# Token products as single float32 products in column strips, coefficients in three bfloat16 parts, with a new table of steps

## The reference, cut to what matters

```python
x = x + 0.5 * ffn(layernorm(x))
x = x + attn(layernorm(x))
x = x + 0.5 * ffn(layernorm(x))

def ffn(x):                                  # x: 4096 tokens x 128
    scores = sigmoid(x @ gate.T)             # 8 experts
    # best of two groups, best two experts in it, coefficients made to sum to 1
    lat = x @ fc1_w.T
    routed = sum over the two experts e of coefficient * (relu2(lat @ w1[e].T) @ w2[e].T) @ fc2_w.T
    return routed + relu2(x @ up_w.T) @ down_w.T      # shared part, 512 wide

def attn(x):                                 # 16 heads of 8
    q, k, v = x @ qkv_w.T                    # q and k turned by position (rotary)
    w = softmax(q @ k.T * SCALE + alibi)
    return (w @ v) @ proj_w.T + proj_b
```

## Time and profile before

| | |
|---|---|
| time, median of 3 runs | 744.61 us (744.25 to 746.72) |
| the profiled execution: its own time | 749.13 us |
| the profiled execution: span of the core | 747.3 us |
| PE busy | 678.4 us (91%) |
| ACT busy | 534.5 us (72%) |
| DVE busy | 436.0 us (58%) |
| POOL busy | 200.2 us (27%) |
| granted TensorE clock, mean | 0.971 |

### The profile page before, as it was taken

The page is one execution under the profiler, slowest core; times in us unless marked ns, Lnnn a source line. Parts: engine busy times, 40 slices in busy tenths (PEclk is TensorE's granted clock), DMA queues, the critical chain, the costliest instruction groups (busy, mean ns, idle before and its releaser), DMA issues.

```text
span 747.3 us, 18920 instructions
## 1 busy us (share of the span) xinstructions
PE 678.4 (91%) x7798; PEld 365.2 (49%) x7798; DVE 436.0 (58%) x1167; ACT 534.5 (72%) x461; POOL 200.2 (27%) x174
## 2 busy tenths in 40 slices
PE   5996999999999989899999999998989899878977
PEld 3884634454454545355535545454445344423556
DVE  4679354667667567648478663673565353424544
ACT  3686487878679677687786695867877787767614
POOL 1116223232432512322425243131132211201130
PEclk9999599999999999999999999999999999988979
DMA  8013512132046140305112301324222000020100
GB/s 263 1 29 112 150 33 68 49 90 61 28 124 155 50 118 6 95 27 142 35 32 51 92 19 44 104 54 108 49 49 62 5 20 6 11 63 6 38 16 19
DMA packets 41024, 46.38 MB, mean 62 GB/s; under 512 B 9186, under 2 KB 27210, under 8 KB 40802
## 3 DMA queue, kind: packets, MB, share of 16 engines
q1 hardware_dynamic: 39122, 43.70, 21.3%
q10 hardware_dynamic: 1808, 1.39, 0.6%
HBM read 25.48 MB, written 19.32 MB: 60 GB/s over the span
## 4 chain that ended last, share of the span: by engine, by line
PE 46%; ACT 15%; DVE 3%; issue 2%; POOL 0%; POOLq 0%; DVEq 0%; ACTq 0%
ACT weights L1415 15%; PE f_acc L1054 13%; PE f_scores L1032 10%; PE f_bank_h L1004 9%; PE f_bank_o L1181 7%; PE f_bank_c L1158 1%; PE f_bank_h L1082 1%; PE f_bank_h L1217 1%; DVE weights L1810 1%; PE f_bank_c L1123 1%; PE f_bank_c L1125 1%; PE f_acc L1181 0%; PE f_bank_c L1134 0%; PE f_bank_h L1113 0%; PE f_scores L1004 0%
## 5 line engine op out<-in xcount | busy, mean ns | idle before, releaser
L1415 ACT ACTIVATE weights<-f_scores 128x2048 f32<-128x2048 f32 (+3 forms) x213 | 394.2, 1851 | 95.8 <-PE f_scores L1032 92.5
L1054 PE MATMUL f_acc<-weights,v_res 128*9 128x512 f32 (+7 forms) x1888 | 230.5, 567 | 2.9 <-DVE f_o_out L1796 2.0
L1032 PE MATMUL f_scores<-q_op,k_full 25*128 25x512 f32 (+8 forms) x1328 | 115.9, 395 | 32.9 <-ACT weights L1415 27.7
L1181 PEld LDWEIGHTS f_bank_o<-w_out,f_hid 128*32 128x32 f32 (+1 forms) x3424 | 109.5, 114 | 73.6 <-issue 70.2
L1810 DVE TENSOR_TENSOR weights<-weights,ediag 128x512 f32<-128x512 f32 x128 | 93.4, 735 | 72.3 <-ACT weights L1415 67.2
L1181 PE MATMUL f_bank_o<-w_out,f_hid 128*32 128x128 f32 (+1 forms) x3424 | 129.0, 276 | 0.0
L1453 POOL TENSOR_TENSOR f_hid<-f_hid,f_relu 128x512 f32<-128x512 f32 x52 | 73.9, 1423 | 161.2 <-DVE f_hid L1669 161.1
L1032 PEld LDWEIGHTS f_scores<-q_op,k_full 25*128 25x128 f32 (+1 forms) x1328 | 56.0, 186 | 108.9 <-ACT weights L1415 74.2
L1453 POOL TENSOR_TENSOR f_hid<-f_relu 128x512 f32<-128x512 f32 x52 | 57.1, 1099 | 166.0 <-ACT f_relu L1328 163.8
L1328 ACT ACTIVATE f_relu<-f_bank_h 128x512 f32<-128x512 f32 x106 | 63.3, 597 | 42.8 <-PE f_bank_h L1004 42.7
L1004 PE MATMUL f_bank_h<-xn_t,w_hi 128*128 128x512 f32 x224 | 85.5, 464 | 3.0 <-DVE xn_t L1569 1.4
(11 more groups left out here) (243 smaller groups left out, 729.0 us busy)
## 6 DMA issues: line engine op xcount, KB each, us to landing
q_parts<-f_parts SPq DMA_DIRECT2D x24, 256.0 KB, 3.0
k_parts<-f_parts SPq DMA_DIRECT2D x24, 256.0 KB, 3.5
q_op<-q_parts SPq DMA_DIRECT2D x48, 96.0 KB
k_full<-k_parts SPq DMA_DIRECT2D x48, 96.0 KB
o_scratch<-f_o_out SPq DMA_DIRECT2D x124, 18.0 KB
x_ln<-in_L_attn_x_dram SPq DMA_DIRECT2D x8, 256.0 KB, 3.9
rope<-const_rope SPq DMA_DIRECT2D x1, 2048.0 KB, 9.2
x_scratch<-f_res SPq DMA_DIRECT2D x8, 256.0 KB, 2.4
```

Source lines behind the costliest of these rows:

```text
L1032: last = nc.tensor.matmul(scores[:, j, at + lo:at + hi], k_full[rows, g, kt * P:(kt + 1) * P], q_op[rows, g, CHUNK * half + lo:CHUNK * hal ...
L1054: last = nc.tensor.matmul(acc[BLOCK * j:BLOCK * j + VW, 0:piece.width], v_res[:, c // HALVES, piece.kt, col:col + VW], weights[:, n % WEIG ...
L1181: last = nc.tensor.matmul(made[strip, t * P:(t + 1) * P], hid[:, m, t * P + strip.start:t * P + strip.stop], w_out[:, m, :], start=(m == 0 ...
L1415: nc.scalar.activation(weights[:, n % WEIGHTS, :, 0:width], scores[:, :, 0:width], ACT.Exp).then_inc(exps_done, 1)
```

## The change

1. A token product is one float32 product, with one copy of the weights (`w_in`) and one of the tokens, in four column strips. The helper `product` makes it. The hidden products, those of queries, keys and values, the gate, the output projection, the spread and all output products (also those of the first two jobs and the last one, which were not cut into strips before) go through it.
2. The low part of the tokens falls away: `take_low` and `take_low2` on DVE, the low copies of the weights in the preparation, and the product of two exponentials (L1575), since the gate's logits come in one piece.
3. The coefficients are spread from three bfloat16 parts (24 rows) in place of two rounded 32-bit parts (16 rows). DVE has two more operations for them, and PE turns them by a bfloat16 product with an identity in place of a transpose.
4. The table of steps is new in all rows.

```diff
-            def times_weights(out, col, x_t):
-
-                for i, (w, part) in enumerate(((w_hi, 0), (w_hi, 1), (w_lo, 0))):
-                    last = nc.tensor.matmul(out, w[:, col:col + P], x_t[:, part, :], start=(i == 0), stop=(i == 2))
+            def product(out, still, moving, start=True, stop=True):
+
+                for strip in STRIPS:
+                    last = nc.tensor.matmul(out[strip, :], still[:, strip], moving, start=start, stop=stop,
+                                            skip_group_check=True)
                 return last
...
                 for t in range(TILES):
-                    at, cols = 2 * EXPERTS * t, slice(t * P, (t + 1) * P)
-                    nc.tensor.matmul(logits[:, at:at + 2 * EXPERTS], x_t[:, 0, cols], w_gate[:, :],
-                                     start=True, stop=False, skip_group_check=True)
-                    last = nc.tensor.matmul(logits[:, at:at + EXPERTS], x_t[:, 1, cols], w_gate[:, 0:EXPERTS],
-                                            start=False, stop=True, skip_group_check=True)
+                    last = product(logits[:, EXPERTS * t:EXPERTS * (t + 1)], x_t[:, t * P:(t + 1) * P], w_gate[:, :])
...
                 for t in range(TILES):
-                    last = nc.tensor.transpose(bank_c[0:2 * EXPERTS, t * P:(t + 1) * P],
-                                               coef_parts[:, t, :].bitcast(F32), ident[:, :])
+                    last = nc.tensor.matmul(bank_c[0:COEF_ROWS, t * P:(t + 1) * P], coef_parts[:, t, :], ident_rows[:, :],
+                                            start=True, stop=True)
...
-                times_weights(hidden_bank(job, m), IN_COL + m * P, normed_t(job)).then_inc(hid_made, 1)
+                at = IN_COL + m * P
+                product(hidden_bank(job, m), w_in[:, at:at + P], normed_t(job)).then_inc(hid_made, 1)
...
-                nc.tensor.matmul(spread_bank(job, m), spread_rows[:, m * P:(m + 1) * P], coef_t[:, :],
-                                 start=True, stop=True).then_inc(spread, 1)
+                product(spread_bank(job, m), spread_rows[:, m * P:(m + 1) * P], coef_t[:, :]).then_inc(spread, 1)
...
-                copy(normed_t(job)[:, 0, :], turn_bank(job)).then_inc(xt_high, 1)
+                copy(normed_t(job), turn_bank(job)).then_inc(xt_ready, 1)
...
-            def take_low(job):
-                dve.wait_ge(xt_high, job.index + 1)
-                v.tensor_tensor(normed_t(job)[:, 1, :], turn_bank(job), normed_t(job)[:, 0, :],
-                                ALU.subtract).then_inc(xt_ready, 1)
...
+                v.tensor_tensor(coef_rest[:, :, :], coef[:, :, :], coef_parts[:, :, 0:EXPERTS], ALU.subtract)
                 v.tensor_tensor(coef_parts[:, :, EXPERTS:2 * EXPERTS], coef[:, :, :], coef_parts[:, :, 0:EXPERTS],
-                                ALU.subtract).then_inc(coef_ready, 1)
+                                ALU.subtract).then_inc(coef_split, 1)
+                dve.wait_ge(coef_split, job.index + 1)
+                v.tensor_tensor(coef_parts[:, :, 2 * EXPERTS:COEF_ROWS], coef_rest[:, :, :],
+                                coef_parts[:, :, EXPERTS:2 * EXPERTS], ALU.subtract).then_inc(coef_ready, 1)
...
-    ("C", 3, dict(front=(355, 359, 360), norm=(361, 365, 366, 368), route=(369, 371, 371, 372, 373), coef=374,
+    ("C", 3, dict(front=(356, 359, 360), norm=(363, 366, 366, 367), route=(368, 368, 368, 368, 368), coef=374,
```

More of the change, by code:

```diff
@@ L810, in normed_t @@
         def normed_t(job):
-            return twin_xn_t if job.twin else xn_t[:, :, :]
+            return twin_xn_t[:, :] if job.twin else xn_t[:, :]
         def relu_tile(job, m):
@@ L1081, in project @@
                 for t in range(TILES):
-                    last = nc.tensor.matmul(bank_h[:, t * P:(t + 1) * P], o_in[rows, t * P:(t + 1) * P], proj_t[rows, :],
-                                            start=True, stop=True)
+                    last = product(bank_h[:, t * P:(t + 1) * P], o_in[rows, t * P:(t + 1) * P], proj_t[rows, :])
                 last.then_inc(proj_made, 1)
@@ L1179, in outputs @@
                 for t in (2 * side, 2 * side + 1):
-                    for strip in ([slice(0, P)] if job.head or job.ends else STRIPS):
-                        last = nc.tensor.matmul(made[strip, t * P:(t + 1) * P],
-                                                hid[:, m, t * P + strip.start:t * P + strip.stop], w_out[:, m, :],
-                                                start=(m == 0 and t == (2 * side if job.ends else 0)), stop=(m == HT - 1),
-                                                skip_group_check=True)
+                    last = product(made[:, t * P:(t + 1) * P], hid[:, m, t * P:(t + 1) * P], w_out[:, m, :],
+                                   start=(m == 0 and t == (2 * side if job.ends else 0)), stop=(m == HT - 1))
                 if side == 1:
@@ L1215, in value @@
                 for t in (2 * side, 2 * side + 1):
-                    for i, (part, w) in enumerate(((0, w_hi), (1, w_hi), (0, w_lo))):
-                        last = nc.tensor.matmul(v_bank(job)[:, t * P:(t + 1) * P], xn2_t[:, part, t * P:(t + 1) * P],
-                                                w[:, col:col + DIM], start=(i == 0), stop=(i == 2))
+                    last = product(v_bank(job)[:, t * P:(t + 1) * P], xn2_t[:, t * P:(t + 1) * P], w_in[:, col:col + DIM])
                 if side == 1:
@@ L1700, in norm2_centre @@
                 last.then_inc(norm2_ready, 1)
-            def take_low2(job):
-                dve.wait_ge(xt2_high, job.chunk + 1)
-                v.tensor_tensor(xn2_t[:, 1, :], out_bank(job), xn2_t[:, 0, :], ALU.subtract).then_inc(xt2_ready, 1)
             def rotary_product(job, i):
@@ L1849, in token @@
                     (last_residual if job.ends else residual)(job)
-                if step == job.at["take_low"]:
-                    take_low(job)
                 if not job.head and step == job.at["take_coef"]:
                     take_coef(job)
-                if job.first and step == job.at["take_low2"]:
-                    take_low2(job)
                 for i in range(5):
@@ L2038, in on_tensor @@
         def on_tensor(pe):
-            def times_weights(out, col, x_t):
-                for i, (w, part) in enumerate(((w_hi, 0), (w_hi, 1), (w_lo, 0))):
-                    last = nc.tensor.matmul(out, w[:, col:col + P], x_t[:, part, :], start=(i == 0), stop=(i == 2))
-                return last
             def project(c):
@@ L2070, in gate @@
                 for t in range(TILES):
-                    for i, (part, at) in enumerate(((0, 0), (1, 0), (0, EXPERTS))):
-                        last = nc.tensor.matmul(ps_g[:, EXPERTS * t:EXPERTS * (t + 1)], x_t[:, part, t * P:(t + 1) * P],
-                                                env["w_gate"][:, at:at + EXPERTS], start=(i == 0), stop=(i == 2))
+                    last = nc.tensor.matmul(ps_g[:, EXPERTS * t:EXPERTS * (t + 1)], x_t[:, t * P:(t + 1) * P],
+                                            env["w_gate"][:, :], start=True, stop=True)
                 last.then_inc(gate_made, 1)
@@ L2079, in turn_coef @@
                 for t in range(TILES):
-                    last = nc.tensor.transpose(ps_g[0:2 * EXPERTS, t * P:(t + 1) * P], coef_parts[:, t, :].bitcast(F32),
-                                               ident[:, :])
+                    last = nc.tensor.matmul(ps_g[0:COEF_ROWS, t * P:(t + 1) * P], coef_parts[:, t, :], ident_rows[:, :],
+                                            start=True, stop=True)
                 last.then_inc(coef_turned, 1)
@@ L2516, in body @@
                     scale(c, m)
-                    if m == 1 and not end:
-                        take_low(c.next())
                 if c.loads_ahead:
```

350 lines of the change are left out of this document (120 added, 230 removed).

## The result

| | before | after |
|---|---|---|
| time, median | 744.55 us (744.25 to 746.72, 4 runs) | 701.73 us (700.5 to 703.51, 4 runs) |
| profiled execution, span | 747.3 us | 701.7 us |
| first exponential starts | 81.54 us | 84.85 us |
| from there to the end of the last exponential | 623.3 us | 580.1 us |
| from there to the end | 42.4 us | 36.8 us |

Between the two profiled executions, 45.6 us apart, the attention gave 43 us, the tail nearly 6, and the head took 3.

The account below looks back on a forecast made before the run. The attention was taken to decide, each step lasting the longer of ACT's exponential and PE's pieces. Attention -23, head +3, tail -3 gave -23 us on 749.1: 726 profiled, median 721, range 706 to 737.

Parts of the forecast that it names:

- 539 + 36 + the same 21 of waits: Attention: ACT's floor 539 us, PE's excess over it 36, waits unchanged at 21; 596 against 623, so -27 us.
- +4 us of new waits: Attention: expert-choice parts sharing a step on DVE delay the diagonal blocks the weighing needs; turns -27 into -23 us.
- Now only the first 9 us are so: Clock in the attention of the old kernel: claimed only its first 9 us run at half clock.
- rival 2: Attention: shorter steps give DVE and POOL chains less cover; if 13 us of waits double, 734 us; chance 0.14.
- less what the shorter chains give back: Attention: dropping low parts shortens each DVE chain between transpose and product by 0.7 us, offsetting some new waits.
- Products and switches: PE in the attention: four-strip products cost 0.86 against 0.69, +21 us; fewer switches between strips and full array, -31.
- Rival 1: Long products: strip weight loads are exposed; 744.6 us or about 755, deciding at 1.09 us per product; chance 0.06.
- The head: Before the first scores: dearer products (+1.3) and more work ahead of the scores at half clock; +3 us in all.
- The tail: After the attention: less work ahead of the last job's choice of experts, against dearer products; -3 us.
- Rival 4: More is gained: -33 us or more, spreads and gates at their cheap ends, no new waits; 708 us; chance 0.1.
- DVE: DVE's work: low parts and L1575 fall, two operations of about 0.25 added per job; 14 us less, not the bound.
- steps like the earlier trace: Against the half-clock rival: ACT-bound steps, PE idle 1.0 of 2.5 us, never lowered the clock between 93 and 660 us.

Follow-up runs that it names:

- full-width run: Changed kernel with hidden, query, key and spread products as one matmul over the full array in place of four strips: 723.2 us, ratio 0.970.
- the run with the subtraction beside the chain: Changed kernel plus 20 DVE subtractions of two static tiles that nobody waits for, in all jobs but the first two: 707.11 us, ratio 0.948.
- the run with the old chains: Changed kernel with old steps for norms, transposes, gates, choice of experts and turned coefficients of the twelve middle jobs: 709.03 us, ratio 0.949.

## Why the prediction was wrong

Its direction held, and so did its account of the prices; its account of the waits did not. Against the profiled execution the forecast was off by 22.6 us (726 for 703.5), 20 of them in the attention (forecast 600 there, 539 + 36 + 21 + 4; measured 580.1) and 2.6 in the tail.

- **The step that failed** is "539 + 36 + the same 21 of waits", with "+4 us of new waits" on top. The 25 became 10.1. Prices account for the other 5: 31 of excess in place of 36, with gate 0.28 (0.64 taken) and spread 0.21 (0.24 taken).
- **I took the remainder for waits that a change of the table does not touch**, and in part it was something else. Of the 16 steps in which I saw PE wait for DVE or POOL, two (1.7 and 1.1 us, at 663 and 678 us) ran at half clock. "Now only the first 9 us are so" was a misreading of the clock row: the 8s of the earlier trace rows are two more stretches of the attention at 1.2 GHz, 660.3 to 667.1 and 677.3 to 684.1. Before, steps at half clock cost 7.3 us, after 3.1. The waits proper fell from 8.0 to 3.0. A wait of this kind is a piece that stands a step too early; a table decides it as much as the evenness does, and I costed only the evenness.
- **Where my fear was right.** With the code alone the waits did grow (8.0 to 12.1, remainder +2.9), as rival 2 said. A choice of experts in one step did block a diagonal block, for 1.0 us. But the table paid for both several times over. That the table alone leaves 13.4, the code alone 24.3, and the pair 10.1 was in none of my cases.
- **What the low parts gave back** I had set at "less what the shorter chains give back", without a number. With the new table it is 5 us in the attention, 3.8 of them waits for a bank.
- **Products and switches** were right: 0.86 for four strips, 0.11 before the scores, no load exposed. Rival 1 falls, its point was 1.09. The rule of the Trainium skill that the prediction cited ("TensorE: Matmul & The Clock Gate", on packing small matmuls), that a weight load overlaps with matmuls in flight only when the row group differs, is not what this trace shows for column strips. The full-width run confirms the switches by themselves.
- **The head** (+3 forecast, +3.3 measured) was right by luck: the same kernel gave -0.6 against before in another trace.
- **The tail** gave 5.6, not 3. I named the earlier gate, but before had two stretches at half clock there, both in the 7 of the clock row, and after had none up to PE's last operation. By the estimate above 4.1 of the 5.6 are clock, and what is left is 1.5. In the runs the tail went with the table (35.8 with the old code), not with the code (41.0).
- **Rival 4** ("more is gained") had the right sign and too little in it: it allowed for no new waits, not for fewer. This also cut the range off at 706.
- **DVE:** I forecast 14 us less. Its busy time fell by 6.4 (436.0 to 429.6), and in the attention by only 1.0 (364.3 to 363.3); the last section shows what took the rest.

What stays open: where the last 5 us of remainder lie that the table takes away with the new code, and why the median of the run with the subtraction beside the chain stands 6 us above after when its trace shows 1.3 in the attention.

## What to carry to other kernels

When a schedule is re-made, cost the waits step by step too: list each wait of before with the piece that is late, look where the new order puts that piece, and only keep the ones that stay. Do not carry a remainder over as a constant. And a cheaper program under an old schedule gives only part of its worth (12.5 of 21.2 us here), since the chains beside it keep their length; code and schedule should be changed, and judged, together.

## What the runs showed of the hardware

**An operation on DVE can be held until POOL's beside it has ended.** With 1 us or so on POOL, even a small one on DVE then lasts that long. In after the operation that opens the choice of experts (L1550, 32 numbers a partition) took 0.97 to 1.39 us in five of sixteen jobs and 0.77 in one more, in the others 0.16 to 0.18. In before another operation stood ahead of it (the product of two exponentials, L1575), and that one was held in the same way in five of sixteen, for 0.72 to 1.07, while L1578, which answers to L1550, took 0.18 in all. Two of the cases of after, on the timeline:

```profile
492.72 1.04 POOL L1433 TENSOR_TENSOR f_hid<-f_relu 128x512 f32<-128x512 f32 x1 [7.77 <-ACT f_relu L1308]
...
492.76 1.03 DVE L1550 TENSOR_SCALAR f_sfc<-f_en 128x32 f32<-128x32 f32 x1 [2.77 <-ACT f_en L1294]
```

```profile
215.52 0.54 POOL L1460 TENSOR_TENSOR f_bound<-f_product,f_half_power 16x1 f32<-16x1 f32 x1
215.72 1.39 DVE L1550 TENSOR_SCALAR f_sfc<-f_en 128x32 f32<-128x32 f32 x1 [0.28 <-ACT f_en L1294]
...
216.04 1.03 POOL L1433 TENSOR_TENSOR f_hid<-f_relu 128x512 f32<-128x512 f32 x1
```

In all five a squaring on POOL runs, and DVE's operation ends 0.04 us after POOL's. In another job, where the squaring began 0.01 us behind it (276.83), it took 0.18. The Trainium skill, "SBUF — State Buffer", section "Who interferes with whom", says that DVE in its mode with two ports and GpSimd exclude each other for a whole instruction, and that the order of issue decides who waits. The trace agrees: at 492.72 POOL was first, and at 215.72 POOL was already at work on `f_bound`, and its next operation went ahead of DVE's too. The start in the record does not always tell who was first: in the run with the subtraction beside the chain, at 424.36, POOL's record starts 0.35 us ahead of DVE's, DVE's lasts 0.68, and it is POOL's that lasts 2.17 in place of 1.57.

This explains the missing fall of DVE's busy time. I counted the operations on DVE that lasted over 0.15 us longer than an undisturbed one (the lower quartile) of their line and shape: 53 in before, 38 us too long in sum; 62 in after, 46 us. Every one of them, in each of the thirteen traces, overlaps an operation on POOL. The 8 us more are what is missing of the 14. It goes with the steps of the chains: 53 operations also in the new code with the old table and in the run with the old chains, 60 to 68 in the others.

**The clock fell after thin steps, and the next full step paid for it.** In after:

```profile
622.60:626.00 3.40, 1.06 (x13) 0.31 (x12) 1.92 (x3) 2.79 (x2) 0.00 (x0) 1.00 0.17 61
626.00:629.40 3.40, 3.30 (x40) 1.82 (x44) 0.69 (x1) 1.92 (x2) 0.00 (x0) 0.55 0.00 0
```

PE was busy for 1.06 of 3.4 us, and then the clock stood at 1.2 GHz from 626.3 to 629.7, in which a full step cost 1.4 us more than its price. PE's longest idle time ahead of it was 1.43 us. I had written that steps like the earlier trace rows never brought the clock down between 93 us and 660 us. Later in the same trace of before three of them in a row stand ahead of a fall:

```profile
670.06:677.30 7.24, 4.51 (x48) 1.27 (x48) 3.11 (x13) 5.39 (x3) 1.01 (x1) 1.00 0.00 0
677.30:684.10 6.80, 6.35 (x32) 1.68 (x32) 2.07 (x3) 4.59 (x4) 0.00 (x0) 0.50 0.00 0
```

Between the runs the number of such stretches in the attention ranged from none to seven, and their cost up to 10.9 us, which makes it a term of its own in a comparison of schedules.
